# When GpSimd forms the weight sums of the fast feed-forward path, and where VectorE adds its second sum

## The reference, cut to what matters

```python
xf = x / 128.0                                    # x: 1024 tokens x 1024
gate = xf @ w_gate.T ; up = xf @ w_up.T           # 2752 rows each, ternary times one scale
inter_q = trunc(clip(silu(gate) * up * 128, -128, 127))
down = inter_q @ w_down.T
out = trunc(clip(down * 128, -128, 127))
x = layernorm(x + out)
```

## Time and profile before

| what | value |
|---|---|
| median of 3 runs | 1541.88 us (1541.4 to 1544.08) |
| the profiled execution | 1543.53 us, span 1541.8 us |
| granted clock of TensorE, mean | 0.992 |
| busy share: PE, DVE, ACT, POOL | 94%, 70%, 48%, 49% |
| start and end of the loop over chunks 3 to 19 on VectorE | 1165.6 and 1431.9 us of the span |
| down product | 1452.7 to 1529.7 us |

### The profile page before, as it was taken

How to read it: one execution, slowest core, us unless ns; L and a number is a source line. 1 busy time by engine, 2 the same in 40 slices (tenths; PEclk the granted TensorE clock), 3 DMA queues, 4 the chain that set the end, 5 groups by cost and what they waited for, 6 DMA issues and landing times. The chain is left out here.

```text
span 1541.8 us, 23361 instructions
## 1 busy us (share of the span) xinstructions
PE 1455.5 (94%) x7332; PEld 1175.1 (76%) x7349; DVE 1085.5 (70%) x1810; ACT 734.2 (48%) x1472; POOL 753.6 (49%) x651
## 2 busy tenths in 40 slices
PE   8899999999999999999999999999789888888896
PEld 6688888888888888888888888876567666666543
DVE  7644444445566677787777777867777888888798
ACT  5433333334444566665656566735642222323374
POOL 0577777776555545555545545535844343333100
PEclk9999999999999999999999999999999999999998
DMA  6477777776744667657576767711312212121511
GB/s 218 165 278 278 277 276 276 273 274 234 237 163 167 248 226 236 244 195 278 170 266 204 252 227 249 241 74 42 123 69 73 78 61 95 61 88 62 203 43 70
DMA packets 105883, 281.11 MB, mean 182 GB/s; under 512 B 12769, under 2 KB 13153, under 8 KB 105825
## 3 DMA queue, kind: packets, MB, share of 16 engines
q1 hardware_dynamic: 105824, 280.41, 52.1%
HBM read 184.94 MB, written 95.42 MB: 182 GB/s over the span
## 5 line engine op out<-in xcount | busy, mean ns | idle before, releaser
L1004 PE MATMUL ps<-xo_h,wb_h 128*128 128x512 f32 x644 | 251.4, 390 | 5.6 <-ACT c L1452 2.4
L1005 PE MATMUL ps<-xo_l,wb_h 128*128 128x512 f32 x644 | 250.6, 389 | 0.0
L1006 PE MATMUL ps<-xo_h,wb_l 128*128 128x512 f32 x644 | 250.6, 389 | 0.0
L1072 PE MATMUL ps<-wo_h,o_h 128*128 128x512 f32 x512 | 206.4, 403 | 0.2 <-DMA wo_l<-wo_low 0.2
L2074 POOL TENSOR_TENSOR pm_l<-pt_l,upto 128x512 fp32r<-128x512 f32 x64 | 82.6, 1291 | 251.0 <-DVE pt_l L2365 251.0
L1073 PE MATMUL ps<-wo_l,o_h 128*128 128x512 f32 x512 | 199.8, 390 | 0.0
L1074 PE MATMUL ps<-wo_h,o_l 128*128 128x512 f32 x512 | 199.6, 390 | 0.0
L1004 PEld LDWEIGHTS ps<-xo_h,wb_h 128*128 128x128 f32 x644 | 120.9, 188 | 33.4 <-issue 6.1
L2047 POOL TENSOR_TENSOR wb_l<-wf_l,wb_h 128x512 fp32r<-128x512 f32 x66 | 87.8, 1330 | 112.5 <-DVE s_sum L2289 56.6
L1006 PEld LDWEIGHTS ps<-xo_h,wb_l 128*128 128x128 f32 x644 | 120.9, 188 | 25.3
L1005 PEld LDWEIGHTS ps<-xo_l,wb_h 128*128 128x128 f32 x644 | 120.9, 188 | 24.8
(11 more groups left out here) (247 smaller groups left out, 3775.0 us busy)
## 6 DMA issues: line engine op xcount, KB each, us to landing
raw<-w_att SPq DMA_DIRECT2D x47, 512.0 KB, 5.5
f_raw<-w_gu SPq DMA_DIRECT2D x44, 512.0 KB, 5.1
u_gu<-f_unit SPq DMA_DIRECT2D x42, 512.0 KB, 4.9
gq<-u_gu SPq DMA_DIRECT2D x42, 512.0 KB, 3.7
wp_raw<-w_att SPq DMA_DIRECT2D x32, 512.0 KB, 5.8
wo_high<-wp_h SPq DMA_DIRECT2D x32, 512.0 KB, 2.8
wo_low<-wp_l SPq DMA_DIRECT2D x32, 512.0 KB, 4.2
q_rows<-c SPq DMA_DIRECT2D x64, 256.0 KB, 2.8
```

The lines of the kernel that those rows point to most:

```text
L1004: pe.matmul(prod_ps[i], wh, chunk(xo_h[i], c), start=(i in OPENS and c == 0), stop=False, skip_group_check=True)
L1005: pe.matmul(prod_ps[i], wh, chunk(xo_l[i], c), start=False, stop=False, skip_group_check=True)
L1006: last = pe.matmul(prod_ps[i], wl, chunk(xo_h[i], c), start=False, stop=(c == KH - 1), skip_group_check=True)
L1072: pe.matmul(into, oh, wo_h[half][:, h, :], start=(h == 0), stop=False)
```

## The change

The GpSimd work is cut in four functions. S3 and S4 get two slots each (`ws` grows from 4 to 6 slots), by the parity of the chunk, so that S3 waits for G7 of two chunks ago and S4 for G3 of two chunks ago. A turn (`sums_between`(n)) now is: wait for VectorE's left product of n-1; S1(n), S4(n); wait for VectorE's left truncation of n-1 to end; S3(n+1); wait for VectorE's right product of n-1; S2(n+1). So S3 and S2 are made one turn ahead, and S3(3) and S2(3) directly after the sums of chunk 2. On VectorE `second_sum2`(n) goes ahead of the left truncation in `chunk_units`; `last_units` keeps its order. For the 4 KB that `ws` takes, `D_NEAR` falls from 8 to 6: six units of the down weights are loaded in the loop and fifteen after G4(20), in `ud_late` parts of 8 and 7.

```diff
-D_NEAR = 8
+D_NEAR = 6
...
-        ws = place("ws", [P, 4, SEQ], F32R, fast(16))
+        ws = place("ws", [P, 6, SEQ], F32R, fast(16))
...
+        def sum_place(parity, k):
+            return {S3_SLOT: parity, S2_SLOT: 2, S1_SLOT: 3, S4_SLOT: 4 + parity}[k]
...
-                with sp.Fori(2, G_LAST // 2) as r:
+                with sp.Fori(2, D_NEAR + 2) as r:
                     for odd in range(2):
                         load_next(r * 2 + odd, odd)
                     load_down(r - 2)
+                with sp.Fori(D_NEAR + 2, G_LAST // 2) as r:
+                    for odd in range(2):
+                        load_next(r * 2 + odd, odd)
...
+            def third_sum(n, parity, loads):
+                pool.wait_ge(gq_loaded[parity], loads)
+                if not isinstance(n, int) or n > G_FIRST + 1:
+                    pool.wait_ge(g_done, g_at(n - 2, G7))
+                pool.tensor_tensor(sum_of(parity, S3_SLOT), weight_quarter(parity, 0, 0), weight_quarter(parity, 1, 0),
+                                   ALU.subtract).then_inc(ws_made, 1)
+            def second_sum(n, parity):
+                pool.wait_ge(ws_made, s_count(n, S3_SLOT))
+                if not isinstance(n, int) or n > G_FIRST:
+                    pool.wait_ge(g_done, g_at(n - 1, G6))
+                pool.tensor_tensor(sum_of(parity, S2_SLOT), weight_quarter(parity, 1, 1), plain(sum_of(parity, S3_SLOT)),
+                                   ALU.subtract).then_inc(ws_made, 1)
+            def first_sum(n, parity):
+                if not isinstance(n, int) or n > G_FIRST:
+                    pool.wait_ge(g_done, g_at(n - 1, G5))
+                pool.tensor_tensor(sum_of(parity, S1_SLOT), weight_quarter(parity, 1, 0), weight_quarter(parity, 1, 1),
+                                   ALU.add).then_inc(ws_made, 1)
+            def fourth_sum(n, parity):
+                pool.wait_ge(ws_made, s_count(n, S2_SLOT))
+                if not isinstance(n, int) or n > G_FIRST + 1:
+                    pool.wait_ge(g_done, g_at(n - 2, G3))
+                pool.tensor_tensor(sum_of(parity, S4_SLOT), weight_quarter(parity, 0, 1), plain(sum_of(parity, S2_SLOT)),
+                                   ALU.subtract).then_inc(ws_made, 1)
+            def sums_between(n, parity, loads):
+                pool.wait_ge(u_product, left(n - 1) + 1)
+                first_sum(n, parity)
+                fourth_sum(n, parity)
+                if loads is not None:
+                    pool.wait_ge(u_signed, left(n - 1) + 1)
+                    third_sum(n + 1, 1 - parity, loads)
+                    pool.wait_ge(u_product, right(n - 1) + 1)
+                    second_sum(n + 1, 1 - parity)
...
                 unit_product(left(n - 1), 1, c_u3[:, :])
+                second_sum2(n, parity)
                 unit_truncate(left(n - 1), 1)
-                second_sum2(n, parity)
                 right_gate(n - 1, 1 - parity)
```

More of the change, by code:

```diff
@@ L212, in build @@
         c_low = place("c_low", [P, SEQ], F32, fast(202))
-        d_near = place("d_near", [P, D_NEAR, DM], BF16, fast(24))
+        d_near = place("d_near", [P, D_NEAR, DM], BF16, fast(28))
         d_far = place("d_far", [P, FC - D_NEAR, DM], BF16, fast(104))
-        lhs = [place(f"lhs{e}", [P, FC, P], BF16, fast(132 + 6 * e)) for e in range(2)]
+        lhs = [place(f"lhs{e}", [P, FC, P], BF16, fast(136 + 6 * e)) for e in range(2)]
         rows2 = place("rows2", [P, TILES, DM], F32, fast(48))
@@ L618, in g_weight @@
                 return gq[parity][:, int(k == G4), half * HALF:(half + 1) * HALF]
-            return ws[:, {G7: S3_SLOT, G6: S2_SLOT, G5: S1_SLOT, G3: S4_SLOT}[k], :]
+            return ws[:, sum_place(parity, {G7: S3_SLOT, G6: S2_SLOT, G5: S1_SLOT, G3: S4_SLOT}[k]), :]
         def t_part(ap, k):
@@ L922, in _ @@
                 for c in range(D_NEAR, FC - 1):
-                    sp.dma_start(d_far[:, c - D_NEAR, :], u_dn[c + 3]).then_inc(ud_late[(c - D_NEAR) // 7], 16)
+                    sp.dma_start(d_far[:, c - D_NEAR, :], u_dn[c + 3]).then_inc(ud_late[(c - D_NEAR) // 8], 16)
                 sp.dma_start(d_far[P - REST:P, FC - 1 - D_NEAR, :], u_dn[FC - 1 + 3][0:REST, :]).then_inc(ud_late[1], 16)
@@ L1283, in down_half @@
                 for c in range(FC):
-                    if first and t == 0 and half == 0 and c in (D_NEAR, D_NEAR + 7):
-                        late = (c - D_NEAR) // 7
-                        pe.wait_ge(ud_late[late], 16 * (7 + late))
+                    if first and t == 0 and half == 0 and c in (D_NEAR, D_NEAR + 8):
+                        late = (c - D_NEAR) // 8
+                        pe.wait_ge(ud_late[late], 16 * (8 + late))
                     last = pe.matmul(bank(D_BANK[k] + half), lhs[k][:, c, :],
@@ L2180, in rest_of_slots, with sum_of @@
                     slot(i, general)
-            def weight_sums(n, parity, loads):
-                g = plain(gq[parity][:, :, :])
-                a11, a12, a21, a22 = g[:, 0, 0:HALF], g[:, 0, HALF:DM], g[:, 1, 0:HALF], g[:, 1, HALF:DM]
-                pool.wait_ge(gq_loaded[parity], loads)
-                if isinstance(n, int) and n == G_FIRST:
-                    pool.wait_ge(x2_kept, 16 * TILES)
-                    pool.wait_ge(x2_turned, TILES)
+            def sum_of(parity, k):
+                return ws[:, sum_place(parity, k), :]
@@ new lines, in weight_quarter @@
+            def weight_quarter(parity, row, half):
+                return plain(gq[parity][:, row, half * HALF:(half + 1) * HALF])
+            def third_sum(n, parity, loads):
+                pool.wait_ge(gq_loaded[parity], loads)
+                if not isinstance(n, int) or n > G_FIRST + 1:
+                    pool.wait_ge(g_done, g_at(n - 2, G7))
+                pool.tensor_tensor(sum_of(parity, S3_SLOT), weight_quarter(parity, 0, 0), weight_quarter(parity, 1, 0),
+                                   ALU.subtract).then_inc(ws_made, 1)
@@ L2195, in weight_sums @@
+            def first_sum(n, parity):
                 if not isinstance(n, int) or n > G_FIRST:
                     pool.wait_ge(g_done, g_at(n - 1, G5))
-                pool.tensor_tensor(ws[:, S1_SLOT, :], a21, a22, ALU.add).then_inc(ws_made, 1)
+                pool.tensor_tensor(sum_of(parity, S1_SLOT), weight_quarter(parity, 1, 0), weight_quarter(parity, 1, 1),
+                                   ALU.add).then_inc(ws_made, 1)
+            def fourth_sum(n, parity):
                 pool.wait_ge(ws_made, s_count(n, S2_SLOT))
-                if not isinstance(n, int) or n > G_FIRST:
-                    pool.wait_ge(g_done, g_at(n - 1, G3))
@@ L2201, in weight_sums @@
-                pool.tensor_tensor(ws[:, S4_SLOT, :], a12, plain(ws[:, S2_SLOT, :]), ALU.subtract).then_inc(ws_made, 1)
+                if not isinstance(n, int) or n > G_FIRST + 1:
[11 more added lines that the diff above has]
+                    second_sum(n + 1, 1 - parity)
@@ L2216, in _ @@
                 rest_of_slots(TILES + 6, False)
-                weight_sums(2, 0, 64)
-                weight_sums(3, 1, 64)
+                pool.wait_ge(x2_kept, 16 * TILES)
+                pool.wait_ge(x2_turned, TILES)
+                third_sum(2, 0, 64)
+                second_sum(2, 0)
+                first_sum(2, 0)
+                fourth_sum(2, 0)
+                third_sum(3, 1, 64)
+                second_sum(3, 1)
+                sums_between(3, 1, 96)
                 with pool.Fori(2, G_LAST // 2) as r:
                     for odd in range(2):
-                        weight_sums(r * 2 + odd, odd, r * 32 + 32)
-                weight_sums(G_LAST, 0, G_LAST // 2 * 32 + 32)
+                        sums_between(r * 2 + odd, odd, r * 32 + (32 + 32 * odd))
+                sums_between(G_LAST, 0, None)
             with pool.Else():
```

## The result

The changed kernel takes 1525.43 us (median of 4 runs, 1524.21 to 1528.36) against 1541.64 for the kernel before in the same comparison: ratio 0.9894, 95% interval 0.9877 to 0.9912. The medians are 16.2 us apart.

The account below looks back on a forecast made before the run. VectorE's chain, lengthened by GpSimd holds, was taken as the bound. Start +1.8, turns -27.2, loop end +1.1, far loads +1.5 and slow clock +1.4 gave -21.4 us from 1541.88: 1520.5 us, 8-in-10 range 1513 to 1531.

Parts of the forecast that it names:

- The holds: In each turn, GpSimd sums and VectorE steps with SBUF operands exclude each other, costing 3.44 us before the change.
- TensorE's idle time before G7: In each turn, TensorE's 1.68 us wait for second_sum2 is an effect of VectorE's lateness, not its cause.
- The rival of a third collision: In each turn, S3(n+1) slips 0.3 us and holds the right product up to 0.97: 1535.7 us, chance 0.12.
- the margin of 0.3 us: Before the right product in each turn: GpSimd's S3(n+1) lets go at T+7.86, the product comes at T+8.15, cost 0.
- S2 was in time: Rival in the loop: S2(n+1), queued behind a chunk load, comes late for G6(n+1); 1556.5 us at 5 us late, chance 0.02.
- The turn: One pass of the chunk loop falls from 15.75 to 14.05 us, gaining 27.2 us over 16 turns.
- My upper bound: For one turn of the loop: 14.55 us, if each GpSimd start is late by 0.25 us.
- The end of the loop: Behind the loop, two held steps delay the add and G7(20); everything to G4(20) is 1.1 us later.
- The far loads: Down-weight loads after G4(20): two more units cost 1.5 us, taken between 1.1 by issue and 2.1 by mean pace.
- The start: Ahead of the loop, S3(3) and S2(3) cause two more holds before a product: +1.8 us, bounds 0 and 2.9.
- The slow clock behind the far loads: After the far loads, 3.5 us of TensorE idle time probably costs 1.4 us at half clock, bounds 0 and 2.8.
- the move as a cost of 0.51 us: Moving the add ahead of the left truncation costs VectorE 0.51 us per turn and pays on TensorE only.

Follow-up runs that it names:

- move_only: The kernel before with second_sum2 moved ahead of the left truncation, GpSimd's order as before: 1524.95 us, ratio 0.9893.
- tail_move: The changed kernel with second_sum2 ahead of the left truncation in last_units too: 1520.03 us, ratio 0.9854.
- no_move: The changed kernel with second_sum2 behind the left truncation again, GpSimd's new order kept: 1527.23 us, ratio 0.9916.
- near4: The changed kernel with D_NEAR 4 in place of 6, two more down-weight units loaded behind G4(20): 1527.31 us, ratio 0.9904.
- start_wait: The changed kernel with S3(3) and S2(3) made to wait for the product of the right half of chunk 1: 1522.23 us in one run.
- start_wait_again: The kernel of start_wait run once more, unchanged: 1521.17 us in one run.

## Why the prediction was right, point by point

It forecast faster, 1520.5 us, range 1513 to 1531; measured 1525.4. The holds, VectorE's chain as the bound, and TensorE's idle time before G7 as an effect were all borne out: seven further kernels placed the sums, the add or the copy otherwise or made the sums short, and their turns were 14.61, 14.52, 12.98, 13.69, 13.14, 14.03 and 12.69 us where the same reckoning, now from the measured 14.28, gave 14.7, 14.6, 13.0, 13.7, 13.1, 14.1 and 12.8 to 12.95. The rival of a third collision didn't come: the right product took 0.75 us. But of the margin of 0.3 us only 0.10 was left, so that the full gain came by little; in move_only this product was held, by 0.28 us. S2 was in time: no wait of G6 for it shows.

Four terms were off in size. Their misses partly cancel: the turn and the end of the loop gave 5.3 us less than said, the far loads and the start 1.95 us more.

- *The turn*, 14.28 for 14.05, 3.7 us in all. I took GpSimd's start at 0.08 us behind VectorE. It was 0.16 for S1 (1282.30 to 1282.46) and 0.27 for S2 (1289.69 to 1289.96); as each hold ends with the sum, that is +0.07 on the left and +0.18 on the right. The moved add came at T+2.91 for 2.78, which cost nothing, as L2761 was held anyway. The trace shows where the lag is larger: in chunks 3 and 20, which stand outside the hardware loop of GpSimd's program, the same sums with the same number of waits start 0.08 us behind VectorE, as predicted, and in every turn inside it 0.16 (S1), 0.24 (S3) and 0.27 (S2). S1(20), behind a product that ended at 1410.59:

```profile
1410.67 1.26 POOL L2215 TENSOR_TENSOR ws<-gq 128x512 fp32r<-128x512 f32 x1 [5.32 <-DVE u_val L2741]
```

So it isn't the number of waits. What in the loop costs it wasn't tested; there the counts waited for are computed from the turn. My upper bound held it.
- *The end of the loop*, +2.7 for +1.1. The add was late as said (G7 at T+6.91, said 7.0). But seven matmuls of G7(20) and G4(20) ran at half clock, 0.43 us apart for 0.23, and two more in part, together 1.6 us; I had priced the clock only at the down product. Before, G2(20) was slow and its slow stretch lay partly in time that would have been waited anyway. That the late add is the cause of the waits is shown by tail_move, which gives back 4.0 us; that S1(20) and S4(20) make it late is read from the two held steps ahead of it. The 1.6 us of slow clock are in part a matter of the execution: in no_move, with the same end, there were none.
- *The far loads*, +0.65 for +1.5: under my lower end in these two profiles. The same stretch differs by about 1 us between profiles with equal loads (near4, above), so whether the term itself was wrong is open.
- *The start*, +0.7 for +1.8: the two holds came (7.29 for 5.40 us between the products), the rest is the length of the slow stretch, 9 matmuls for 13, and start_wait shows that this length differs between executions of one kernel. That is luck.

The slow clock behind the far loads cost 1.6 us for 1.4, but in start_wait_again, after a longer idle time, nothing: that this term fits is luck too.

The Trainium skill (SBUF — State Buffer, Who interferes with whom) has it that issue order decides who blocks; the rows agree: S3 at 1287.69 lay beside an add from PSUM and idle time, and held nothing; S2 at 1289.96 was issued before L2761 at 1290.39 and held it.

What the prediction didn't ask is how the parts add. The move alone gives 1.23 us a turn, GpSimd's new order alone 1.14, both 1.47, not 2.37: both move the sums away from the same truncation steps, and the holds that one has removed the other can't remove again. I priced the move as a cost of 0.51 us that pays on TensorE only. In the kernel before it was worth 1.23 net, since it let S3 start earlier.

## What to carry to other kernels

Where one step takes two lengths in a regular loop, look which other engine is busy beneath the long ones: here an operation on GpSimd and a VectorE step with all operands in SBUF excluded each other, and only where the sums, the add and the copy stood, not how many they were, was worth 2.6 us in a turn of 15.8. List the stretches of a turn in which VectorE reads PSUM or waits, and give each at most one GpSimd operation that fits in whole; then ask of every edit that shifts a release what it does to those placements, for gains of edits that remove the same collision don't add. Price the turn, and the last turn separately: there the same collision had nothing to hide behind.

## What the runs showed of the hardware that I had not expected

- A held VectorE step ends as if it had begun 0.15 us before the end of the GpSimd operation, to within 0.02 us for steps of 0.43 and 0.69 us; the product of 0.75 us in move_only ended 0.05 us earlier than that.
- GpSimd started 0.16 to 0.27 us behind the VectorE instruction that it waited for in every turn of its hardware loop, and 0.08 us behind it with the same waits in the chunks outside the loop (3 and 20).
- After the same idle time of 5.5 us, one kernel's matmuls ran at half clock (1.2 GHz) 6 times in one execution and 13 times in the next. After 3.0 us of idle time in the changed kernel G2(20) ran at full clock for all of its eight matmuls and the clock fell only later, within G7(20); after 2.57 us in the kernel before G2(20) was slow at once, and so it was after 3.02 us in start_wait_again, whose end is the changed kernel's.
